# A two-layer sequence model on one core: how its attention layer starts up, and the order of its first feed-forward products

## The reference, cut to what matters

```python
# layer 0: norms, a style vector per entry, then a mixture of 8 experts, the 2 best of each token
x = x + combine(top2(router(h)), experts(h))
# layer 1, 16 heads of 16 columns, feed-forward width 1024
x = _ln(x) * (1.0 + scale) + shift
q, k, v = x @ Wq + bq, x @ Wk + bk, x @ Wv + bv
scores = einsum('bhqd,bhkd->bhqk', q / 4, k) + attention_bias; scores = where(src_mask, -inf, scores)
x = x + softmax(scores) @ v @ Wo + bo
h = _ln(x) * g2 + beta2
return x + _gelu2(h @ W1 + b1) @ W2 + b2          # _gelu2(x) = x * sigmoid(1.702 x)
```

## Time and profile before

| | us |
|---|---|
| median of 3 runs (1447.22 to 1448.72) | 1448.05 |
| the profiled execution, its own time | 1434.4 |
| its span in the trace | 1432.6 |
| layer 0, up to the barrier | 0 to about 622 |
| start-up of layer 1, up to the first `minimum` | about 622 to 672 |
| sixteen entries and the end | about 672 to 1433 |

### The profile page before, as it was taken

One profiled execution on the slowest core, in us unless ns is written; L12 is line 12 of the kernel. 1 busy time (PEld: TensorE's weight loads), 2 busy tenths in 40 slices (PEclk: granted clock), 3 DMA queues, 4 the chain that ended last, 5 costly groups with the idle time before them and its releaser, 6 DMA issues. The chain is left out here.

```text
span 1432.6 us, 34478 instructions
## 1 busy us (share of the span) xinstructions
PE 1273.8 (89%) x9923; PEld 1165.2 (81%) x9923; DVE 990.3 (69%) x2766; ACT 899.0 (63%) x2318; POOL 664.5 (46%) x580
## 2 busy tenths in 40 slices
PE   5874899999999999935799999899998999999996
PEld 4774899999999999934587888778887877788875
DVE  5776788879887888646565667666765667666652
ACT  3442777778777877711666676666665666667661
POOL 2775577777777777742132332322332232331211
PEclk9999999999999999967999999999999999999998
DMA  5885121221112112146766555655665556654620
GB/s 194 270 269 188 43 65 48 57 63 55 55 49 64 55 47 65 42 153 196 226 200 200 178 180 192 215 185 171 185 205 185 171 180 204 203 189 149 192 68 15
DMA packets 184851, 203.18 MB, mean 142 GB/s; under 512 B 18192, under 2 KB 172752, under 8 KB 184720
## 3 DMA queue, kind: packets, MB, share of 16 engines
q1 hardware_dynamic: 170832, 163.14, 36.8%
q10 hardware_dynamic: 7712, 21.89, 4.8%
q0 software_dynamic: 6176, 16.79, 3.3%
HBM read 155.89 MB, written 41.68 MB: 138 GB/s over the span
## 5 line engine op out<-in xcount | busy, mean ns | idle before, releaser
L1224 ACT ACTIVATE bias<-bias,neg_max 128x256 f32<-128x256 f32 x512 | 255.4, 501 | 207.6 <-DVE neg_max L1536 207.0
L343 POOL TENSOR_TENSOR w_lo<-w,w_hi 128x512 fp32r<-128x512 f32 x156 | 241.2, 1567 | 0.0
L1536 DVE CUSTOM_DVE_ANT_0 bias<-ps_s,bias 128x256 f32<-128x256 f32 x512 | 194.3, 417 | 28.6 <-PE ps_s L1312 11.1
L745 DVE TENSOR_TENSOR w_lo<-w,w_hi 128x512 fp32r<-128x512 f32 x156 | 149.9, 1000 | 70.2 <-ACT w_hi L423 68.6
L544 PE MATMUL ps_y<-w_hi,hidT_hi 128*128 128x256 f32 x624 | 180.1, 289 | 1.9 <-DVE token_rows L759 1.9
L531 PE MATMUL ps_h<-htokT_hi,w_hi 128*128 128x256 f32 x624 | 178.4, 286 | 3.2 <-DVE htokT_lo L750 3.2
L1310 PE MATMUL ps_s<-mask_f,minus_ident 128*128 128x256 f32 x512 | 154.9, 324 | 28.5 <-DVE neg_max L1536 16.3
L1176 POOL TENSOR_TENSOR act_lo<-up_f,act_hi 128x512 fp32r<-128x512 f32 x64 | 82.6, 1290 | 208.4 <-ACT act_hi L1268 208.4
L531 PE MATMUL ps_h<-htokT_lo,w_hi 128*128 128x256 f32 x624 | 178.2, 286 | 0.0
L531 PE MATMUL ps_h<-htokT_hi,w_lo 128*128 128x256 f32 x624 | 178.0, 285 | 0.0
L544 PE MATMUL ps_y<-w_hi,hidT_lo 128*128 128x256 f32 x624 | 177.1, 284 | 0.0
(11 more groups left out here) (271 smaller groups left out, 3546.9 us busy)
## 6 DMA issues: line engine op xcount, KB each, us to landing
bias<-bias_dram SPq DMA_DIRECT2D x128, 512.0 KB, 4.2
w<-w_dram ACTq DMA_DIRECT2D x32, 512.0 KB, 5.3
xin<-dispatch SPq DMA_DIRECT2D x39, 256.0 KB, 2.7
expert_out<-token_rows SPq DMA_DIRECT2D x39, 256.0 KB, 2.2
q_stack<-q_hi_rows SPq DMA_DIRECT2D x64, 128.0 KB, 3.0
k_stack<-k_hi_rows SPq DMA_DIRECT2D x64, 128.0 KB, 2.9
q_stack<-q_lo_rows SPq DMA_DIRECT2D x64, 128.0 KB, 2.9
k_stack<-k_lo_rows SPq DMA_DIRECT2D x64, 128.0 KB, 2.8
```

The lines of the kernel that those rows point to most:

```text
L343: pool.tensor_tensor(w2_part["lo"][:, k, :], w2_piece(e, k), w2_part["hi"][:, k, :].bitcast(F32), ALU.subtract).then_inc(sem("w2_split"), 1)
L745: dve.tensor_tensor(w1_part["lo"][:, k, :], w1_piece(e, k), w1_part["hi"][:, k, :].bitcast(F32), ALU.subtract).then_inc(sem("w1_split"), 1)
L1224: act.activation(head_rows(h, j), head_rows(h, j), ACT.Exp, scale=-1.0, bias=neg_max[par][:, h, j:j + 1], accum_out=total[par][:, h, j:j + ...
L1536: dve.tensor_tensor_reduce(head_rows(h, j), ps_s[h % 2][:, j * T:(j + 1) * T], head_rows(h, j), -1.0, LARGEST, ALU.add, ALU.min, neg_max[p ...
```

## The change

It has four parts.

1. **First stacks on two queues.** The parts of entry 0 no longer go through `send_parts` and `bring_stacks` of SP. A new `first_stack` runs on SP for q and on ScalarE for k: each sends two parts and brings eight stacks, with semaphores of its own. SP issues chunks 1 to 3 of the bias right behind. VectorE clears `q_stack[0]` first and then both `v_pad`; ScalarE clears `q_stack[1]` by an activation with scale 0.
2. **Feed-forward weights loaded behind the stacks, prepared in the first entries.** ScalarE issues W1, b1, bo, b2 and wo (`load_layer`) after the k stacks, and W2 (`load_w2`) at head 14 of entry 0, into the buffers that held W1. The folding and splitting is spread over VectorE's heads 6 and 9 to 13 of entry 0 (W1) and 2 and 3 of entry 1 (W2). `fold_norm` of TensorE stands behind head 8 of entry 0 and uses the banks `ps_out` and `ps_k`.
3. **Second entry combined sooner.** In step -1 VectorE combines and normalises entry 1 right after the values of entry 0; TensorE and ScalarE transpose and modulate it at head 7 of step -1 instead of head 15.
4. **Rounded passes first.** In `feed_up` a tile's four products with the rounded input come first and the two with the rest last; the wait for `hT_split` stands behind the first four.

```diff
-    b1_row = probT[:, 0:2, :, :].rearrange("p h j t -> p (h j t)")
-    less_gain = probT[:, 2, :, :].rearrange("p j t -> p (j t)")[:, 0:C * P].rearrange("p (c m) -> p c m", c=C)
-    w1_raw = [buf[:].rearrange("p f t -> p (f t)") for buf in (up_f, tanh_f)]
-    w2_raw = [buf[:].rearrange("p j d -> p (j d)") for buf in (ctxT, x3, x3b, h_rows)]
+    ps_fold = [ps_out, ps_k]
+    b1_row = [buf[:].rearrange("p j d -> p (j d)") for buf in (x3, x3b)]
+    less_gain = h_rows[:].rearrange("p j d -> p (j d)")[:, 0:C * P].rearrange("p (c m) -> p c m", c=C)
+    raw = [buf[:].rearrange("p f t -> p (f t)") for buf in (up_f, tanh_f)]
...
+    def first_stack(eng, which):
+        eng.wait_ge(sem(f"{which}_split"), 2 * C)
+        for piece in ("hi", "lo"):
+            name = f"{which}_{piece}"
+            eng.dma_start(io[name].rearrange("(m p) t -> p m t", p=P), part[name][:].bitcast(F32)).then_inc(sem(f"{which}_sent"), 16)
+        eng.wait_ge(sem("q_zeroed0"), 1)
+        eng.wait_ge(sem(f"{which}_sent"), 32)
+        for term in range(len(PASS_ROWS)):
+            for i in range(2):
+                dst, src = stack_rows(which, term, i, 0)
+                eng.dma_start(dst, src).then_inc(sem("stack_in"), 16)
...
-            sp.wait_ge(sem("split_sent"), 64 * (n + 1))
+            sp.wait_ge(sem("split_sent"), 64 * n)
             if isinstance(n, int) and n < 2:
-                sp.wait_ge(sem("q_zeroed"), n + 1)
+                sp.wait_ge(sem("q_zeroed1"), 1)
...
-                send_parts(n + 1)
+                if starting:
+                    first_stack(sp, "q")
+                    for c in range(1, RING):
+                        load_bias(n + 1, c)
+                else:
+                    send_parts(n + 1)
...
-            if exists(n + 1):
+            if exists(n + 1) and not starting:
...
+        act.activation(q_stack[1][:].bitcast(F32R), spread(const[:, ONES:ONES + 1], [P, H, T], 1), ACT.Copy, scale=0.0).then_inc(sem("q_zeroed1"), 1)
+        def load_layer():
+            for c, dst in enumerate(raw):
+                act.dma_start(dst, io["ff_w1"][:, c, :]).then_inc(sem("fold_in"), 16)
+            for i, dst in enumerate(b1_row):
+                act.dma_start(dst, io["ff_b1"][i * 512:(i + 1) * 512].partition_broadcast(P)).then_inc(sem("fold_in"), 16)
+            for i, dst in enumerate((bo, b2)):
+                act.dma_start(dst[:], io["rows"][1 + i].partition_broadcast(P)).then_inc(sem("layer_in"), 16)
+            act.dma_start(wo[:], io["wo"]).then_inc(sem("layer_in"), 16)
+        def load_w2():
+            act.wait_ge(sem("w1_lower"), C)
+            for i, dst in enumerate(raw):
+                act.dma_start(dst, io["ff_w2"][:, 4 * i:4 * i + 4, :].rearrange("p f d -> p (f d)")).then_inc(sem("w2_in"), 16)
...
-                if isinstance(n, int) and n == 0 and h == 10:
-                    act.wait_ge(sem("setup_done"), 2)
+                if isinstance(n, int) and n == 0 and h == 14:
+                    load_w2()
+                if isinstance(n, int) and n == 1 and h == 8:
+                    act.wait_ge(sem("w2_lower"), 2)
...
-                if exists(n + 2) and h == 15:
+                if exists(n + 2) and h == (7 if starting else 15):
...
+                    if starting and h == 6:
+                        first_stack(act, "k")
+                        load_layer()
...
-                pe.wait_ge(sem("hT_split"), n + 1)
+                pe.wait_ge(sem("hT_upper"), n + 1)
                 if exists(n + 2):
                     pe.wait_ge(sem("v_ready"), J * (n + 3))
             elif pair >= 2:
                 pe.wait_ge(sem("gelu_ready"), 4 * n + pair - 1)
             for i in range(2):
                 f = 2 * pair + i
+                sums = ps_up[pair % 2][:, i * T:(i + 1) * T]
                 for c in range(C):
-                    for k, (a, b) in enumerate(PASSES):
-                        last = pe.matmul(ps_up[pair % 2][:, i * T:(i + 1) * T], w1[a][:, c, f * P:(f + 1) * P], hT_part[b][:, c, :],
-                                         start=(c == 0 and k == 0), stop=(c == C - 1 and k == 2))
+                    for a in ("hi", "lo"):
+                        pe.matmul(sums, w1[a][:, c, f * P:(f + 1) * P], hT_part["hi"][:, c, :], start=(c == 0 and a == "hi"), stop=False)
+                if f == 0:
+                    pe.wait_ge(sem("hT_split"), n + 1)
+                for c in range(C):
+                    last = pe.matmul(sums, w1["hi"][:, c, f * P:(f + 1) * P], hT_part["lo"][:, c, :], start=False, stop=(c == C - 1))
...
+            pe.wait_ge(sem("k_split"), 2 * C * 2)
             for i in range(2):
                 for c in range(C):
-                    last = pe.matmul(ps_p[i][:, :], less_gain[:, c, :], w1_raw[c][:, i * 512:(i + 1) * 512],
+                    last = pe.matmul(ps_fold[i][:, :], less_gain[:, c, :], raw[c][:, i * 512:(i + 1) * 512],
...
-                if isinstance(n, int) and n == 1 and h == 0:
-                    pe.wait_ge(sem("setup_done"), 2)
+                if isinstance(n, int) and n == 0 and h == 8:
+                    fold_norm()
+                if isinstance(n, int) and n == 0 and h == 15:
+                    pe.wait_ge(sem("fold_taken"), 1)
+                if isinstance(n, int) and n == 1 and h == 3:
+                    pe.wait_ge(sem("layer_in"), 16 * 3)
+                if isinstance(n, int) and n == 1 and h == 7:
+                    pe.wait_ge(sem("w1_lower"), C)
+                if isinstance(n, int) and n == 1 and h == 11:
+                    pe.wait_ge(sem("w2_lower"), 2)
...
-                    if isinstance(n, int) and n == -1 and h == 6:
-                        fold_norm()
...
-            for i, bank in enumerate(ps_p):
-                last = dve.tensor_tensor(b1_row[:, i * 512:(i + 1) * 512], bank[:, :], b1_row[:, i * 512:(i + 1) * 512], ALU.add)
+            for i, bank in enumerate(ps_fold):
+                last = dve.tensor_tensor(b1_row[i], bank[:, :], b1_row[i], ALU.add)
...
-            s.then(dve.tensor_scalar(b1_row, b1_row, 1.0 / D, None, ALU.mult))
+            for i in range(2):
+                last = dve.tensor_scalar(b1_row[i], b1_row[i], 1.0 / D, None, ALU.mult)
...
+        def fold_w1(c):
+            for i in range(2):
+                cols = raw[c][:, i * 512:(i + 1) * 512]
+                dve.scalar_tensor_tensor(cols, cols, vec[:, LN2_G + c:LN2_G + c + 1], b1_row[i], ALU.mult, ALU.add
+                                         ).then_inc(sem("w1_folded"), 1)
+        def split_w1(c):
+            dve.wait_ge(sem("w1_folded"), 2 * (c + 1))
+            dve.tensor_copy(w1["hi"][:, c, :], raw[c]).then_inc(sem("w1_rounded"), 1)
+            dve.wait_ge(sem("w1_rounded"), c + 1)
+            dve.tensor_tensor(w1["lo"][:, c, :], raw[c], w1["hi"][:, c, :].bitcast(F32), ALU.subtract).then_inc(sem("w1_lower"), 1)
+        def w2_rows(piece, i):
+            return w2[piece][:, 4 * i:4 * i + 4, :].rearrange("p f d -> p (f d)")
+        def split_w2(i):
+            dve.wait_ge(sem("w2_in"), 16 * 2)
+            dve.tensor_scalar(w2_rows("hi", i), raw[i], 0.5, None, ALU.mult).then_inc(sem("w2_rounded"), 1)
+            dve.wait_ge(sem("w2_rounded"), i + 1)
+            dve.scalar_tensor_tensor(w2_rows("lo", i), raw[i], 0.5, w2_rows("hi", i).bitcast(F32), ALU.mult, ALU.subtract
+                                     ).then_inc(sem("w2_lower"), 1)
+        def split_weights(n, h):
+            if n == 0:
+                if h == 6:
+                    prepare_fold()
+                if h == 9:
+                    fold()
+                if 10 <= h < 12:
+                    fold_w1(h - 10)
+                if 12 <= h < 14:
+                    split_w1(h - 12)
+            elif n == 1:
+                if 2 <= h < 4:
+                    split_w2(h - 2)
...
+                if isinstance(n, int) and n == -1 and h == 6:
+                    combine_first(n + 2)
+                    combine_second(n + 2)
+                    input_moments(n + 2)
+                    normalise(n + 2)
+                elif exists(n + 2) and not (isinstance(n, int) and n == -1):
...
+        dve.memset(q_stack[0][:], 0.0).then_inc(sem("q_zeroed0"), 1)
         for i in range(2):
             dve.memset(v_pad[i][:], 0.0).then_inc(sem("v_zeroed"), 1)
-            dve.memset(q_stack[i][:], 0.0).then_inc(sem("q_zeroed"), 1)
...
```

63 lines of the change are left out of this document (21 added, 42 removed).

## The result

The changed kernel takes 1427.11 us (median of 4 runs, 1426.71 to 1428.88), the kernel before in the same comparison 1447.63 (1445.57 to 1448.72). The ratio is 0.9871 [0.9846, 0.9896], so 1.3% faster (20.5 us between the medians, 18.7 by the ratio); 1436.3 was forecast, with 1428 to 1443. The direction is as forecast, but the gain is larger by more than half. The profiled execution of the changed kernel took 1427.18 us (span 1425.4). That is like its other runs, while the profiled execution of before was 13.65 us shorter than its others. So between the two profiles only 7.2 us are gained, less than the 11.7 forecast; between the runs it is about 20. The rest of this document is about both gaps.

The account below looks back on a forecast made before the run. TensorE's own stream (89% busy) was taken to bound the batch, a dependency chain the start. Terms -5.2 (start), -5.0 (part 4) and -1.5 gave -11.7, so 1422.7 us profiled; with 13.65 us added, 1436.3, range 1428 to 1443.

Parts of the forecast that it names:

- Carried over from one profile to the runs: Whole kernel: the profile's 13.65 us below the median of runs was assumed to hold after the change too.
- Clearing: Start: without a buffer clearing ahead of it, VectorE combines entry 0 as its rows land, 2.6 us earlier.
- Two queues: Start: q and k stacks issued on separate queues bring the first scores 4.4 us earlier, beyond the clearing.
- third rival: Start: DMA engines hold the stacks, scores at 663, 4 us later than forecast; 1440.3 us in all, chance 0.07.
- VectorE: Start: with weight preparation moved away, the first minimum follows the first scores by about 1 us, gaining 4.7 us.
- Paid back in entry 0: Heads 6 to 13: inserted folding and splitting of W1 costs 6.3 us after cover, bounds 3 and 10.
- first rival: Entry 0: insertion costs its upper bound, 10 us, as TensorE's clock may fall; 1441.5 us in all, chance 0.15.
- split of W2: Entry 1, heads 2 and 3: VectorE's split, twice 2.1 us, priced at 0.2 us because VectorE waits there.
- Part 4: feed_up: rounded products fill the wait for hT_lo, 0.26 to 0.3 us an entry, 5 us over 16 entries.
- The clock: TensorE's clock: a gain of 1.5 us in the sum.
- second rival: Entry 0 and clock: 3 us paid back, clock -5 as most low stretches vanish; 1429.5 us in all, chance 0.20.
- The slower case: Whole kernel: the change makes it slower, chance 0.05.

Follow-up runs that it names:

- e5: The changed kernel unaltered, run again beside the kernel before: 1426.01 us, ratio to before 0.9893.
- e1: The kernel before, unchanged, profiled again: 1433.07 us, ratio to before 0.9993.
- e4: The changed kernel with SP's bias chunks 1 to 3 and ScalarE's weight loads waiting for all sixteen stacks: 1425.32 us, ratio to before 0.9934.
- e8: The changed kernel with SP's bias chunks 1 to 3 and ScalarE's weight loads ahead of the stacks: 1428.72 us, ratio to before 0.9905.
- e10: The changed kernel with bias chunk 1 behind chunk 0, chunks 2, 3 and all weight loads on SP behind the stacks: 1423.61 us, ratio to before 0.9926.
- e2: The kernel before with part 4 alone (rounded passes first in feed_up): 1427.99 us, ratio to before 0.9951.
- e3: The changed kernel without part 4, so parts 1 to 3 alone: 1430.41 us, ratio to before 0.9970.
- e11: As e10, but with all sixteen stacks and their parts on SP's one queue: 1424.42 us, ratio to before 0.9931.
- e9: The kernel before, unchanged, profiled again in the set of e9 to e12: 1434.69 us, ratio to before 0.9998.
- e7: The kernel before with five throwaway matmuls of TensorE ahead of feed_up's wait for hT_lo: 1430.16 us, ratio to before 0.9914.
- e12: As e10, with throwaway matmuls of TensorE added in the start: 1425.20 us, ratio to before 0.9941.
- e6: The kernel before with part 1 alone (new clearing order, two stack queues): 1438.96 us, ratio to before 0.9981.

## Why the prediction was partly right

**Carried over from one profile to the runs: the step that failed.** I put the 13.65 us by which the profile before lies below its runs on the changed kernel as well. It doesn't have them: its profile and runs agree, and in e5 it takes 1426.0 us again, while the kernel before takes 1434.5, 1441.1 and 1447.6 in different sets. The rule that what I see no cause for stays equal was the error.

What the 13 us are is shown only in part. From the set of e1 to e4 to that of e5 to e8 the kernel before gets 6.4 us slower. The stall can make some 3.5 of it (eight periods are 0.3 to 0.6 us longer in e5 than in e4). Clock makes about 1.4: the mean clock of its runs is 0.9706 in the first set and 0.9696 in the second. The rest is open. The changed kernel has the stall as well, but its clock is higher where the stall is (0.975 in e5, 0.976 in the first comparison; e4 and e10, without the stall, have 0.973 and 0.972). Of the runs at 1447.6 us neither a profile nor a clock is on record, so their further 6.6 us, and why the changed kernel is free of them, stay open.

**The sum for a chip like that of the profile: near.** -11.7 was forecast; e2 and e3 add up to -10.9. That is in part luck: among the terms, errors cancelled.

- *Clearing*, -2.6: 2.5 measured.
- *Two queues*, -4.4: wrong in the changed kernel, where they brought nothing. The first scores came 2.5 us earlier, as much as the clearing gives, and so they did in e5, though k's product, which took 3.06 us in the first profile, took 1.95 there; in both the last k stacks land 6.3 us after their issue. The step that failed took only the sixteen stacks and a stretch by 0.18 into account and left the bias and weights "right behind" to a clause. The queue that is done first goes on to its next loads (SP's bias chunks from 655.43), and these run against the other queue's stacks (ScalarE issues until 657.1, and they land 6.3 us after issue; 4.8 in e10). e11 and e10 show the 4.4 us without them. The third rival (scores at 663) was right on the place: over 654 to 664 us the share is 1.11, and the issue time saved was gone. Without the loads behind, in e11 and e10, 5.0 us of issue were saved and 4.4 us gained.
- *VectorE*, -4.7: 4.4 (from scores to first `minimum` 5.7 us before, 1.2 after).
- *Paid back in entry 0*, +6.3: 4.5. From first `minimum` to that of entry 1 it took 38.1 us and takes 42.6. The wait for the bias is gone as foreseen. TensorE's clock fell there, as the first rival feared (10.2 us of low clock between 696 and 712, 3.4 before), and even so it came out below the forecast. From there to `hT_lo` of entry 0, with the split of W2 in between, it takes 25.2 us instead of 24.7, so 0.6 lost against 0.2 forecast; but e9, the unchanged kernel, has 25.2 as well. `hT_lo` of entry 0: relative 108.0 instead of 110.0, so 2.0 us where 5.2 were forecast (3.2 in e5). e3 as a whole gains 4.3, more than that. Some of it fits the clock (10.2 us low between 720 and 1340, against 13.6 to 20.4); no run isolates it.
- *Part 4*, -5.0: 0.05 us an entry instead of 0.3, so 0.8 us in all. The wait went as foreseen and the new one came as foreseen, at 0.21. The mis-sized step is the bound: I let the transposition start 0.06 us behind the end of the exponential, at 829.72. But each exponential has a read of its accumulator behind it, 0.19 us, and in the trace the transposition starts only behind that read. In the changed kernel it ends at 872.74 and the transposition starts at 872.87, 0.13 later. It is so in all ten entries that run in the loop (0.13 us behind the read, 2.63 from `hT_lo`); in five that are written out it is 0.05 behind the read, the delay that I had put behind the exponential itself, and 2.56 from `hT_lo`. So the ceiling was 0.11 us an entry in the loop and 0.18 outside; where the rest of it went wasn't traced.
- *The clock*, -1.5: no run shows this term, which was my estimate. What the runs showed in its place is the real content of part 4: an estimated 5 us in the set of e2 (6.7 us in all, about 1 of it from the shorter periods), and more on the chip with the stall (e7: 10.9 with nothing shortened). The second rival had -5 for it and was right on this point.

**The slower case**, at 0.05 among the chances, that two short pauses let the clock fall in every entry, was wrong: with pauses of 0.23 and 0.21 us it falls in none of the entries between 720 and 1340 in the two profiles of the changed kernel, and in two to four in those of e2, e4, e8, e10, e11 and e12, which have the new order too. The profiles with the old order have three to five, e6's nine. So with the long pause there are as many low stretches here or more.

**The signs named.** Combination near 633: yes, 633.38. First scores at 658.5 to 660: no, 663.9. First `minimum` at 660: no, 665.1, and "stacks that land 4 us or more after their last issue" was on the list of what would show it wrong; it was 6.8. No wait for the bias of head 14: yes. First `minimum` of entry 1 5 to 6 us earlier: no, 2.5 (relative 82.7 instead of 85.3). Wait for `hT_lo` down from 16.0 to 5: more than that, no matmul waits for it, but they wait 4.2 us for `hT_hi`, which I hadn't counted. A period 0.3 shorter: no, 0.05.

## What to carry to other kernels

The pause of TensorE ahead of `feed_up` cost here more than its own length: e7 filled it without shortening it (the first real product stands 0.74 us behind the start of `hT_lo`, before 0.75) and took 10.9 us less. So price a pause by the low stretches of the clock in its neighbourhood, and try a filler first: it took five throwaway products here, and the mean clock of four runs (0.979 against 0.970) told what the clock was worth. When a burst of transfers is spread over two queues, look at what each queue issues next. Here the first scores stood at relative 39.0 with loads right behind the stacks, and at 36.2 in e10, where the loads wait for the other queue's stacks too. Ask also which engine such a wait stands on: on ScalarE it cost the start again (e4: first exponential at 667.65), on SP it didn't (e10: 664.58). And if a profile lies a per cent below the runs, ask which of the two kernels will show that difference: here the kernel before took between 1434.4 and 1447.6 us, the changed one 1426.0 and 1427.1.

## What the runs showed of the hardware

- ScalarE sat idle for 0.16 to 0.62 us ahead of its copy of head 2 in eight or nine of sixteen entries, in the first profile after and in the four profiles of e5 to e8 (one chip). In the same entries of the eight profiles of the two other chips, and of the profile before, the copy starts without idle time (0.08 to 0.10 us ahead of the recorded end of the read before it). e7's ScalarE runs the same program as that of before. No dependency that the trace shows was late.
- The kernel before ran at medians of 1434.66, 1441.05, 1434.44 and 1447.63 us in four comparisons. Its single runs spread by 6.2 us (e1 to e4), 10.2 us (e5 to e8: 1435.16 to 1445.35, with clocks from 0.966 to 0.973) and 6.9 us (e9 to e12) in the three sets; the kernels with the pause filled or shortened by 1.6 us (e7) to 6.0 us (e5).
- From 654 to 658 us of e4, where only stacks (128 KB each, into 16 partitions) are issued or still landing, the DMA engines moved 242 and 233 GB/s at shares of 1.10 and 1.13. From 646 to 648 us of the kernel before, where weight loads and gathered rows are under way and no part of q or k is sent yet, they moved 369 GB/s at 1.03.
- The granted clock fell to 0.50 for 3.4 us at a time (6.8 at 778 us, in before and e1) at the cluster of pauses around the first product of `feed_up`. In the old order these are 0.78, 0.40 and 0.96 us (before: ahead of 1008.78, 1009.89 and 1011.50), and the clock falls at about 1011.0, inside the last; at 778.9 (before) it falls ahead of the last already. In all profiles the stretches between 720 and 1340 us begin between 0.8 us ahead of the start of `hT_lo` and 1.3 us behind it. There are five of them in before and e9, three in e1 and e3, and nine in e6. With 0.23 us in place of 0.96, and 0.21 ahead of the next transposition, there are none in after and e5 and two to four in e2, e4, e8, e10, e11 and e12. With the pause filled down to 0.36 us (e7) there are none.
- A float32 matmul of 256 columns is two rows in the trace of e12: 72 throwaway matmuls are 144 rows, and rows of this kind follow each other every 0.22 us at a granted clock of 1.00. So the filler was twice as many rows as I had counted.
